# A two-layer graph network on one core: part of the MLP's first product made during layer 0's edge loop

## What is computed

```python
# layer 0
msg  = relu(x[src] + edge_attr_64 @ W_e + b_e)
h    = (1 + eps) * x + segment_sum(msg, dst)
h    = silu(bn(h @ W1 + b1, g1, beta1))     # W1: 512 x 1024; bn over the 1250 nodes
h    = silu(bn(h @ W2 + b2, g2, beta2))     # W2: 1024 x 512
x    = layernorm(x + h)
# layer 1
m    = relu(concat(x[src], edge_attr_128) @ V1.T + v_b1) @ V2.T + v_b2
agg  = segment_sum(m, dst)
x    = layernorm(x + (x + batchnorm(gru(agg, x))))
```

## Time and profile before

| | |
|---|---|
| median of 3 runs | 835.72 us |
| profiled execution | 837.82 us |
| its span | 836.2 us, 11420 instructions |
| TensorE matmuls | 775.3 us (93%), 3734 |
| TensorE weight loads | 629.5 us (75%) |
| VectorE | 637.1 us (76%) |
| ScalarE | 449.3 us (54%) |
| GpSimd | 360.0 us (43%) |
| layer 0's edges | up to 233 us |
| MLP | 235 to 348 us |

### The profile page before, as it was taken

One profiled execution on the slowest core, in us unless ns is written; L12 is line 12 of the kernel. 1 busy time (PEld: TensorE's weight loads), 2 busy tenths in 40 slices (PEclk: granted clock), 3 DMA queues, 4 the chain that ended last, 5 costly groups with the idle time before them and its releaser, 6 DMA issues.

```text
span 836.2 us, 11420 instructions
## 1 busy us (share of the span) xinstructions
PE 775.3 (93%) x3734; PEld 629.5 (75%) x3734; DVE 637.1 (76%) x1126; ACT 449.3 (54%) x809; POOL 360.0 (43%) x382
## 2 busy tenths in 40 slices
PE   7879998888999999798599999999999999999995
PEld 5556665555679999677377878787778998989895
DVE  7779999898989826388599999999986372626255
ACT  4879998888854403211377777787763121111122
POOL 7777777777600000023677777777730000000011
PEclk9999999999999999989799999999999999999998
DMA  8999988888630050014578888888831220200011
GB/s 227 318 300 305 274 265 261 245 250 242 197 102 1 1 202 0 1 38 144 173 250 298 265 257 259 258 260 265 261 115 39 76 76 1 76 1 1 1 51 72
DMA packets 49389, 134.38 MB, mean 161 GB/s; under 512 B 8265, under 2 KB 8521, under 8 KB 48944
## 3 DMA queue, kind: packets, MB, share of 16 engines
q0 software_dynamic: 26720, 87.58, 34.2%
q1 hardware_dynamic: 22116, 45.59, 17.0%
q10 hardware_dynamic: 492, 0.45, 0.2%
HBM read 128.47 MB, written 5.12 MB: 160 GB/s over the span
## 4 chain that ended last, share of the span: by engine, by line
PE 57%; POOL 11%; DVE 11%; DMA 10%; issue 7%; ACT 3%; SPq 0%; DVEq 0%; POOLq 0%; ACTq 0%
PE banks L519 39%; POOL raw L448 11%; PE banks L546 9%; DMA raw<-in_x,src_sb 6%; PE banks L576 3%; PE banks L577 3%; DVE msg_lo L1115 3%; DVE raw L1123 2%; DMA x_in<-in_x 2%; DMA raw<-table_dram,src_sb 2%; DVE hot L1109 1%; ACT banks L854 1%; DVE attr_lo L1038 1%; PE banks L590 1%; PE banks L599 1%
## 5 line engine op out<-in xcount | busy, mean ns | idle before, releaser
L448 POOL DMA_INDIRECT raw<-in_x,src_sb x167 | 168.9, 1011 | 54.2 <-issue 43.9
L448 POOL DMA_INDIRECT raw<-table_dram,src_sb x167 | 162.8, 975 | 61.1 <-issue 36.6
L470 POOL TENSOR_TENSOR moments<-moments,minus_half 128x1 f32<-128x1 f32 x32 | 20.3, 636 | 304.0 <-DVE moments L1258 304.0
L1123 DVE TENSOR_TENSOR raw<-banks,raw 128x512 f32<-128x512 f32 x168 | 114.3, 681 | 21.5 <-PE banks L546 16.9
L854 ACT ACTIVATE banks<-raw 128x512 f32<-128x512 f32 x166 | 99.0, 597 | 58.6 <-DMA raw<-table_dram,src_sb 33.5
L898 ACT ACTIVATE msg_hi<-raw 128x512 fp32r<-128x512 f32 x168 | 104.8, 624 | 31.9 <-DVE raw L1123 29.1
L1115 DVE SCALAR_TENSOR_TENSOR msg_lo<-raw,msg_hi 128x512 fp32r<-128x512 f32 x168 | 114.3, 680 | 6.3 <-ACT msg_hi L898 6.1
L576 PE MATMUL banks<-msg_hi,hot 128*128 128x512 f32 x293 | 115.9, 395 | 0.8 <-DVE agg L1138 0.4
L577 PE MATMUL banks<-msg_lo,hot 128*128 128x512 f32 x293 | 114.6, 391 | 0.0
L546 PE MATMUL banks<-We_hi,attr 97*128 97x512 f32 x167 | 86.4, 517 | 17.2 <-ACT banks L854 15.4
L1115 DVE SCALAR_TENSOR_TENSOR msg_lo<-banks,msg_hi 128x512 fp32r<-128x512 f32 x125 | 84.7, 678 | 1.4 <-ACT msg_hi L898 1.3
(11 more groups left out here) (171 smaller groups left out, 1726.1 us busy)
## 6 DMA issues: line engine op xcount, KB each, us to landing
attr_sb<-in_attr SPq DMA_DIRECT2D x84, 128.0 KB, 4.5
attr_sb<-in_attr SPq DMA_DIRECT2D x42, 256.0 KB, 4.0
Wg_raw<-in_Wg SPq DMA_DIRECT2D x3, 1536.0 KB, 6.2
raw<-in_x,src_sb POOLq DMA_INDIRECT x167, 4.9
raw<-table_dram,src_sb POOLq DMA_INDIRECT x167, 4.1
x_in<-in_x SPq DMA_DIRECT2D x5, 512.0 KB, 14.4
rows<-in_x SPq DMA_DIRECT2D x1, 2560.0 KB, 12.2
table_dram<-table_sb SPq DMA_DIRECT2D x9, 256.0 KB, 2.0
```

What stands on the lines that cost most here:

```text
L448: pool.indirect_dma_start(rows_of(L, t), None, tables[L], bass.IndirectOffsetOnAxis(ap=src_sb[:, t:t + 1], axis=0)).then_inc(gathered[t % ...
L470: nc.gpsimd.tensor_tensor(moments[:, slot * 4 + 2:slot * 4 + 3], moments[:, slot * 4 + 1:slot * 4 + 2], minus_half[:, 0:1], ALU.pow).then_ ...
L1123: nc.vector.tensor_tensor(rows_of(L, t), edge_bank(t), rows_of(L, t), ALU.add).then_inc(added[L], 1)
```

## The change

The first 512 nodes (`FIRST`) have all their edges in the first six groups (`FIRST_GROUPS`), that is in steps up to 35. From step 40 ScalarE and VectorE split the sums of these nodes (`first_hi`, `first_lo`). From step 44 to 85 TensorE adds two matmuls of 512 columns to each step: twelve in six steps make one block's product for these nodes, in bank 7, for seven blocks; the eighth block's twelve matmuls stand behind the loop, where the 20 transposes were. VectorE evicts each into `first_h0`, adding the bias, and only after the eighth goes to `agg_done`. All 8 blocks of W1 are split in VectorE's edge loop, one every six steps from 38 on.

In the MLP the first product has only the chunks of 384 and 354 nodes. SiLU is three calls for a block: from `first_h0` into `pre`, again from `first_h0` straight into `s_hi`, and over the other 738 nodes of `pre`; the cast on VectorE covers these 738 alone. W2 comes in four DMAs, each into the place of two blocks of `first_h0` once these have been used, and one block of it is split by VectorE in each of c = 3 to 7, three more behind the last hidden split. The second product's six early accumulators go input by input, each as soon as it is split. The groups from the seventh on have their window at node 512 at least, and if edges are left, the first 512 nodes' product is made again after them.

```diff
+FIRST = NODE_CHUNKS[0][1]
+FIRST_GROUPS = 6
+HIGH_AT, LOW_AT, PRODUCTS_AT, PRODUCT_STEPS = 40, 41, 44, 6
+PASSES = 3 * KD
+SPLIT_W1_AT = 38
...
-            sp.wait_ge(agg_start, BLOCKS)
-            sp.wait_ge(add_mm[0], TILES)
-            sp.dma_start(W2_raw[:, :, :], W2.rearrange("(k p) n -> p k n", p=P)).then_inc(w2_in, 16)
+            for i in range(KH // 2):
+                sp.wait_ge(first_used, 2 * i + 2)
+                sp.dma_start(W2_raw[:, 2 * i:2 * i + 2, :], W2[2 * i * P:(2 * i + 2) * P, :].rearrange("(k p) n -> p k n", p=P)
+                             ).then_inc(w2_in[i], 16)
...
+            def first_passes(m, parts):
+                ms = slice(m * P, (m + 1) * P)
+                for p in parts:
+                    k, i = divmod(p, 3)
+                    if p == 0:
+                        pe.wait_ge(w1_split, m + 1)
+                        if m == 0:
+                            pe.wait_ge(flag_ready, 1)
+                        else:
+                            pe.wait_ge(first_out, m)
+                    if m == 0 and i == 0:
+                        pe.wait_ge(agg_low[0], k + 1)
+                    W, X = ((W1_hi, first_hi[:, k, :]), (W1_hi, first_lo[k][:, :]), (W1_lo, first_hi[:, k, :]))[i]
+                    mm = nc.tensor.matmul(first_bank[:, 0:FIRST], W[:, k, ms], X, start=p == 0, stop=p == PASSES - 1)
+                    if p == PASSES - 1:
+                        mm.then_inc(first_mm, 1)
...
+                    if L == 0 and first_part(j):
+                        m, part = first_part(j)
+                        each = PASSES // PRODUCT_STEPS
+                        first_passes(m, range(part * each, (part + 1) * each))
...
-            keep_busy(20)
+            first_passes(KH - 1, range(PASSES))
...
-                each = [(m, q) for m in range(M) for q in range(3)]
+                each = [(m, q) for m in range(M) for q in mlp_chunks(0 if K == KD else KH)]
                 early = 6 if K == KH else 0
                 if early:
+                    for k in range(K - 2):
+                        pe.wait_ge(w2_split, k + 1)
+                        pe.wait_ge(s_split, k + 1)
+                        for i, (m, q) in enumerate(each[:early]):
+                            if k == 0:
+                                pe.wait_ge(mlp_out, n + i - 5)
+                            product(bank[2 + (n + i) % 6][:, 0:NODE_CHUNKS[q][1]], terms(m, q, [k]), start=k == 0, stop=False)
                     pe.wait_ge(w2_split, KH)
-                    pe.wait_ge(s_split, KH - 2)
-                    for i, (m, q) in enumerate(each[:early]):
-                        pe.wait_ge(mlp_out, n + i - 5)
-                        product(bank[2 + (n + i) % 6][:, 0:NODE_CHUNKS[q][1]], terms(m, q, range(K - 2)), stop=False)
...
+                if c < KH:
+                    normalized(pre[:, c % 2, 0:FIRST], first_h0[:, c, :])
+                    normalized(s_hi[:, c, 0:FIRST], first_h0[:, c, :]).then_inc(first_used, 1)
+                    normalized(pre[:, c % 2, FIRST:N], pre[:, c % 2, FIRST:N]).then_inc(silu_done, 1)
...
+            def first_bias(m, acc):
+                return nc.vector.tensor_scalar(first_h0[:, m, :], acc[:, 0:FIRST], vec("b1", m), None, ALU.add)
+            def first_evict(m):
+                dve.wait_ge(first_mm, m + 1)
+                first_bias(m, first_bank).then_inc(first_out, 1)
...
+                    if L == 0 and PRODUCTS_AT < j and (j - PRODUCTS_AT) % PRODUCT_STEPS == 0:
+                        first_evict((j - PRODUCTS_AT) // PRODUCT_STEPS - 1)
...
+                if L == 0:
+                    first_evict(KH - 1)
                 leftover(L)
...
-                split(s_hi[:, c, :], s_lo[:, c, :], pre[:, c % 2, :]).then_inc(s_split, 1)
+                link(nc.vector.tensor_copy(s_hi[:, c, FIRST:N], pre[:, c % 2, FIRST:N]))
+                low_part(s_lo[:, c, :], pre[:, c % 2, :], s_hi[:, c, :]).then_inc(s_split, 1)
...
-                if c + W1_FIRST < KH:
-                    split_w1(c + W1_FIRST)
+                if 3 <= c < KH:
+                    split_w2(c - 3)
                 rstd_now()
```

112 lines of the change are left out of this document (80 added, 32 removed).

## The result

| | |
|---|---|
| median of the changed kernel | 847.94 us (4 executions) |
| the kernel before, beside it | 836.19 us (833.18 to 836.75) |
| ratio, 95% interval | 1.0135 (1.0094 to 1.0175) |
| its profiled execution, its span | 844.13 us, 842.3 us |

The change makes the kernel slower, by 1.35% (0.94 to 1.75%). One of the four executions took 1427 us, and none of the later runs of any kernel was like it: the ratio leaves it out, the median of 847.94 doesn't, and the middle one of the other three is 844.13. Between the profiled executions the difference is 6.3 us (844.13 against 837.82), between the medians 11.8 (7.9 with the 1427 us left out). The profiled one of before lies 1.6 over its median, that of the changed kernel 3.8 under its own.

What follows compares the result with a forecast made beforehand. The prediction took TensorE to bound the MLP, with the blocks' chain 0.4 us under it, and nobody to be full in layer 0's second half. 4.9 + 2.9 - 4.7 + 2.0 = +5.1 us gave a median of 840.8, range 832 to 849.

Steps and rivals of the forecast that it cites:

- 1, layer 0's second half: Layer 0's edge loop, steps 44 to 85: 2.72 us a step against 2.60 for 40 steps, +4.9 us (bounds +1.6 and +16).
- 2.2 + 0.3 = 2.5 a step: Layer 0's second half: VectorE's present work plus the change's added work per step in us, under TensorE's 2.64.
- the 97% assumed: Layer 0's second half: TensorE busy 97% with the change, making its 2.64 us a step 2.72.
- 2, the end of layer 0: Between layer 0 and the MLP: twelve matmuls and an eviction delay the first copy, +2.9 us (bounds 2.4 and 3.5).
- 3, the MLP: From the sums' first copy to the second product's end: 106.7 us against 111.4, -4.7 us (bounds -8 and -1).
- 4, the clock: Second product's opening: TensorE's clock is low after little work, +2 us (bounds 0 and +4).
- The 3 us more: MLP's first product: by the skill's rule blocks 3 to 5 cost 1 us more each, the sum 3 us higher.
- A: Rival, layer 0 absorbs the added work, step under 2.65 us, and the clock holds: not slower, 835 us; chance 25%.
- B: Rival, MLP: TensorE stays the limit, blocks' chain at 4.1 us: faster, 821 us (830 at 6.0 a block); chance 10%.
- C: Rival, layer 0's loop: VectorE's seven lumps are passed on, TensorE at 93%: +15, at most 850 us; chance 15%.
- D: Rival: edges of the first 512 nodes lie past group 6, so the left-edge path runs; chance under 1%.

Runs made afterwards that it cites:

- e4: Changed kernel with seven evictions and the eight W1 casts moved from VectorE to ScalarE in layer 0's edge loop: 846.43 us, ratio 1.0127.
- e3: Changed kernel with seven more 512-column VectorE additions that nobody reads, one every six steps of layer 0's edge loop: 850.06 us, ratio 1.0182.
- e2: Changed kernel with the moved matmuls of seven blocks on 128 instead of 512 columns, VectorE's work unchanged: 843.77 us, ratio 1.0107.
- e5: Changed kernel with the loop's moved matmuls on 128 columns, and seven evictions and eight W1 casts given to ScalarE: 843.47 us, ratio 1.0097.
- e1: Changed kernel with the eighth block's matmuls behind the left-edge branch and their eviction behind the sums' low parts: 842.35 us, ratio 1.0092.
- e6: Changed kernel with unread matmuls before the waits of the second product's early accumulators, to hold the clock up: 842.76 us, ratio 1.0092.
- e0: The changed kernel run again as it is, the control for the experiments: 846.31 us, ratio 1.0147 to the kernel before.
- e11: Changed kernel with evictions and statistics reordered in the MLP and the eighth block's product moved behind, on a slow chip: 949.79 us, ratio 0.9996.
- e9: Kernel before with only the MLP's evictions and statistics reordered, on a chip where the kernel before took 939 us: 937.18 us, ratio 0.9975.

## Why the prediction was right or wrong

The forecast, slower with TensorE's gain lost in a chain of blocks, is what happened; its size was 3 to 7 us short (840.8; measured 847.9, or 844.1 with the 1427 us left out), within the range. By its own parts:

**1, layer 0's second half, +4.9. Size right by luck, reason half wrong.** I put TensorE at 2.72 us a step with its waits. From the addition at 115.77 to that at 229.13 lie 42 steps: 2.70 each; before, 116.60 to 224.88, 2.58 each. That is +5.1, and with the last interval (10.6 against 9.5) +6.3; measured by the absolute marks, +5.4. TensorE's own 2.64 a step fits e4 (15.8 for six). What failed is the sentence "That is 2.2 + 0.3 = 2.5 a step: under TensorE". The price of 0.58, an average of layer 1's window over 166 long and 7 short instructions, is not that of this mix: it is 0.60, 0.66 and 0.72, together 15.65 us for six steps, 2.61 and not 2.5. So VectorE stands beside TensorE (e3). It sets the first two intervals, 17.1 and 16.6, as e2 (unchanged there) and e4 (2.1 us less) show: the four low parts of the sums fall in them, three and one, at 0.6 each, which I had spread over 48 steps. From the third on the loop runs at 2.65, 99.5% of TensorE's pace, better than the 97% assumed. Two errors of some 2 us cancelled. I had also put 11.2 us of waits for placement down as room that fills up; they did go, but the kernel before ran its middle intervals at 15.65, and e5 doesn't get below that with both engines lighter.

**2, the end of layer 0, +2.9.** Measured +3.3 in the trace, and 2.9 by e1. The first copy moved by 8.7, forecast "about 8". That the order of these matmuls costs as much wasn't said, and isn't so: e1 takes the 2.9 away and gets 0.5 to 2.2 of it at the last SiLU.

**3, the MLP, -4.7. The term that failed.** The chain of blocks is the limit, as argued; first SiLU at 9.55 after the first copy (9.7 forecast). But a block takes 7.1 and 7.4, not 6.8 and 7.2. The step is "the new three calls (512, 512, 738) are 0.67 + 0.67 + 0.90 less 0.09 overlap twice, 2.05". The 0.67 for 512 columns was taken from the minimum of the second row, a group of six calls of four shapes. The minimum belongs to the 354-column call. The rows of the kernel before tell it once its shapes are kept apart (mean ns behind the comma), and so does its timeline; below them the calls of the kernel after:

```profile
L953 ACT ACTIVATE y_t<-pre,moments 128x512 f32<-128x512 f32 x1 | 0.8, 814 | 2.3 <-DVE moments L1297 2.3
...
L953 ACT ACTIVATE y_t<-pre,moments 128x354 f32<-128x354 f32 x1 | 0.7, 670 | 0.0
```

```profile
349.51 1.99 ACT L953 ACTIVATE y_t<-pre,moments 128x512 f32<-128x512 f32 x3 [2.26 <-DVE moments L1297]
```

```profile
L1022 ACT ACTIVATE pre<-first_h,moments x8: 813/816/817, 253.5 to 304.7; 128x512 f32<-128x512 f32 x8
L1022 ACT ACTIVATE s_hi<-first_h,moments x8: 799/802/804, 254.2 to 305.4; 128x512 fp32r<-128x512 f32 x8
L1022 ACT ACTIVATE pre<-pre,moments x8: 987/989/992, 255.0 to 306.2; 128x738 f32<-128x738 f32 x8
```

The three calls at 349.51 cover 512, 384 and 354 columns, 1250 together, in 1.99 us where one call takes 1.43: a warning that stood in the trace. 512 columns are 0.82, 738 are 0.99, and the three calls take 2.43 from start to end, not 2.05. The W2 split costs 0.30 a block, not 0.45. Together the SiLU of block 6 starts 53.35 us after the first copy instead of 52.1. The second product ends at 110.5 (300.23 + 54.28 - 243.97): from before's 111.4 that is -0.9, where parts 3 and 4 together gave -2.7.

**4, the clock, +2.** Measured by e6 as 2.2 to 2.4. It was right in place, kind and size. The rule of the Trainium skill (TensorE: Matmul & The Clock Gate, on HAM oscillation), that groups behind pauses begin slowly, agrees with the trace as far as the opening goes: behind a wait of 4.08 us before 285.43 the clock was 0.58, and then 0.50 up to 304. The 3 us more that I worked out if the blocks themselves ran at the low clock did not come. The reason is that TensorE made nearly the whole first product in one piece, ahead of the blocks' chain (to 275.99), and had ended it at 280.3, before the clock fell at 284. So no run here tests the rule on the blocks.

By the traces then: 5.4 + 3.3 - 0.9 = +7.8 where the last SiLU stands (measured +7.9), where the parts gave +5.1; 1.8 is given back behind it in one trace (842.3 - 357.4 = 484.9 against 486.7) and not in e0 (486.8), so it is scatter. The medians differ by 11.8 and 11.5, with intervals from 7.9 on. With the 1427 us left out the first of them is 7.9, which the traces cover. What is over 8 in e0 lies in executions without a profile, and I can't place it.

**The rivals.** A (the loop absorbs it) falls by its own sign, a step under 2.65 us: it is 2.70 over the 42 steps. But it was nearer than its chance says, since the five middle intervals run at 2.65 and took in 14 us of matmuls for 1.4. B needed the chain to run at 4.1 us; it does 7.4. But the argument that the order on VectorE forbids it was too strong: with another order it runs at 5.49, and the second product starts 45.6 us after the first copy (339.14 - 293.50) instead of 56.3. C is right in the engine and wrong in form: VectorE's work is passed on in the first two intervals (3.7 us), not in seven lumps. D didn't occur: the chain has nothing of a left-edge loop.

## What to carry to other kernels

Work that is moved out of a full stretch pays only as far as the chain beside it lies lower: here the second chain was 0.4 us a block below TensorE, so that the MLP became 0.9 us shorter for 22.4 us of TensorE taken out, while the loop and its end became 8.7 longer. Such a move wants the chain shortened first, here by making the next block's statistics before the last block's split; with that the MLP gave 12 us, but the whole kernel was only level with the one before on the two chips where it was run. Price every engine that the moved work touches by start-to-start distances of its own shapes: a minimum or a mean of a row with several forms belongs to none of them. And shortening the way to one mark is no gain by itself: look whether the chain behind it starts earlier too.

## What the runs showed of the hardware

- A SiLU call has a fixed part that matters at these sizes. Durations are 0.82 us for 512 columns, 0.99 for 738 and 1.43 for 1250; two further calls for the same columns cost 0.56 us (1.99 against 1.43).
- VectorE's start-to-start distance for 512-column instructions is 0.60 us, and 0.72 both into and out of one that works on 64 partitions. What causes the 0.12 wasn't looked into.
- A gap of 2.5 us before the MLP was followed by the low clock (0.52 over 3 us) in e0, and by the full clock in the first trace. It cost 1.5 us. The matmuls ahead of the gap were twelve of 512 columns without a pause in both, so what decides it isn't in these rows. In five of the nine traces with this gap the clock fell.
- The same kernel took 835 to 836 us on some chips and 939 to 950 on two others. The traces of the slow ones have "remote" waits of up to 11.6 us on VectorE (e11), and the granted clock of e9 was 0.86 in the window 130 to 230.
